# Moving the between-layer steps inside the attention loop of a two-layer kernel from eight places per phase to two

## The chip, the cores and the metric

The kernel runs on one core of a Trainium2 chip. The time is the device time of one execution in microseconds (us). The kernel before has a median of 1164.96 us over three runs (1164.99, 1161.2 and 1164.96).

## The reference, cut to what matters

The program is a stack of four blocks with a residual sum around each: attention, a mixture of experts, a state-space block and a second mixture of experts. Only the end of attention and what feeds the first mixture of experts matter here.

```python
x = x + attention(layernorm(x))            # 2 batches of 1024 tokens, 128 wide, 16 heads of 64
x = x + experts0(layernorm(x))             # below
x = x + state_space(layernorm(x))
x = x + experts1(layernorm(x))

def attention(x):
    Q, K, V = x @ W_Q + b_Q, x @ W_K + b_K, x @ W_V + b_V
    return softmax(Q @ K.T / 8) @ V @ W_O + b_O

def experts0(x):
    logits = (x @ wg_red.T) @ wg_unit.T                 # 8 experts
    scores, e = max(softmax(logits)), argmax(logits)    # one expert a token
    return scores * (gelu(x @ w1[e] + b1[e]) @ w2[e] + b2[e])
```

## The kernel before, in words

Attention is worked in 16 pairs of heads, pairs 0 to 7 for the first batch and 8 to 15 for the second. A pair has two phases, c = 0 and c = 1, one for each half of its 1024 queries. Every engine runs its own instructions strictly in the order of one list of steps, which `whole_order` writes out; a step is a name such as ("score", 3, 0, 5), and each engine takes from the list the steps in which it has a part. So a step's place in the list is its place on TensorE (PE), VectorE (DVE), ScalarE (ACT), GpSimd (POOL) and in the queue of SyncE (SP) at once. The line numbers below are those of the kernel before.

One phase, written by the function `phase`, is this:

- A head of eight rounds. In each, PE makes one product for the maxima of the next pair ("max", L605), which DVE reduces (L1507), and one block of scores of this pair ("score", L589 and L593), whose exponentials ACT takes (L1078). Maxima go through two slots of PSUM in turn and scores through two others. So the product for maxima number j has to wait until DVE has reduced number j-2, and the scores number j until ACT has taken the exponentials of number j-2. One of the two slots for maxima contains bank 7.
- A tail. PE multiplies the eight blocks of exponentials with the values ("pv" 0 to 7, L621). Between these products stand small steps: keys and queries of the pair after the next ("proj", L637, then k_lo or q_lo on DVE, L1500), in phases c = 1 a transposed row of maxima ("row", L660), the values of the next pair ("values", L652, taken by DVE with `valued`, L1536), and the sums of the softmax ("sumhalf", L671, taken by DVE, L1548). All of these use one bank of PSUM, bank 7, and each waits until the one before it has been read. "take" at the end is ACT's copy of the output to SBUF (L1087).
- POOL adds up the exponentials (L2020), seven additions a phase, all through the head and the tail; in the order of the list they come with the scores.

Into this loop the kernel also puts steps of the blocks around it: the layer norm of the second batch before attention (n = 1) and of the first batch before the experts (n = 2), and the routing of the first batch. Their parts are these.

- `lnvar` is 8 BN_STATS and 8 BN_AGGR on DVE (L1458, L1462). `lnroot` is four small instructions on POOL (L1967 to L1975). `lnrows` is 8 activations on ACT that write xrows (L1096), and it waits for `lnroot`. `lnturn` is 4 transposes on PE (L575) into bank 7, and `lncopy` reads them with ACT (L1040).
- `xr` is a matmul on PE (L703) into bank 7 and a copy on ACT; `logits` is 8 matmuls (L714) into bank 7, and `choose` six dependent instructions on DVE (L1603 to L1613), the second of which frees bank 7.
- `total` is 9 matmuls on PE (L725, L727) into bank 7. `count` in three parts (L1629 to L1660) is chains on DVE that end in the row numbers and the owners of slots. `scatter` is two indirect DMAs that POOL issues (L2031). `rate` is two small instructions on DVE.
- `rows`, `turn`, `turned` and `fetch` load the scattered rows, transpose them (PE into bank 7, then an ACT copy) and fetch the experts' weights (DMAs from SP's queue).

The table `EARLY` names the place of each such step. Before, its key is (pair, c, j): the steps go behind pv number j of that phase, j being one of 1, 3, 5, 6 and 7, and 7 meaning behind "take". `phase` puts them there as beside[1], beside[3] and so on. A second table, `LAST_EARLY`, does the same for the four pieces of the last pair.

Of the kernel before, what the change touches and what calls it, by code (L numbers as in the profile page):

```python
# [164 lines left out]
EARLY = {(3, 0, 1): [("lnvar", 1), ("lnroot", 1)], (3, 1, 3): [("lnrows", 1)], (4, 0, 5): [("lnturn", 1, 0), ("lncopy", 1, 0)],  # L165
         (4, 1, 6): [("lnturn", 1, 1), ("lncopy", 1, 1)], (5, 0, 1): [("bias", 1)],
         (8, 1, 1): [("lnvar", 2), ("lnroot", 2)], (9, 0, 3): [("lnrows", 2)], (9, 1, 6): [("lnturn", 2, 0), ("lncopy", 2, 0)],
         (10, 0, 5): [("lnturn", 2, 1), ("lncopy", 2, 1)], (10, 1, 6): [("xr", 0, 0), ("xr_out", 0, 0)], (11, 0, 5): [("xr", 0, 1), ("xr_out", 0, 1)],
         (11, 1, 1): [("logits", 0), ("choose", 0)], (12, 0, 1): [("expo", 0), ("alog",), ("total", 0), ("count", 0, 0)],
         (12, 0, 3): [("count", 0, 1)], (12, 1, 1): [("count", 0, 2)], (12, 1, 3): [("scatter", 0, 0), ("rate", 0)],  # L170
         (13, 0, 1): [("scatter", 0, 1)], (13, 0, 3): [("scatter", 0, 2)], (13, 0, 7): [("scatter", 0, 3)],
         (13, 1, 7): [("rows", 0, 0), ("rows", 0, 1)], (14, 0, 1): [("fetch", 0)], (14, 0, 5): [("turn", 0, 0), ("turned", 0, 0)],
         (14, 0, 7): [("fetch", 1), ("rows", 0, 2)], (14, 1, 1): [("fetch", 2)], (14, 1, 6): [("turn", 0, 1), ("turned", 0, 1)],
         (14, 1, 7): [("fetch", 3), ("rows", 0, 3)]}
# [2354 lines left out]
```

## Time and profile before

| what | value |
|---|---|
| median of three runs | 1164.96 us |
| the profiled execution | 1164.99 us |
| its span on the core | 1163.7 us |
| PE busy | 1096.0 us, 94% |
| DVE busy | 835.9 us, 72% |
| ACT busy | 619.0 us, 53% |
| POOL busy | 761.6 us, 65% |
| granted TensorE clock, mean | 0.985 |

The profiled execution took 1.3 us more than its span. Attention fills the span from about 45 to 734 us. In a row of the timeline the first number is the start in us from the span's start, the second the time from there to the end of the group, and what stands in brackets is how long the engine had been idle before it and what ended that. The clock is 1.00 at TensorE's level of 2.4 GHz and 0.50 at 1.2 GHz.

### The profile page before, as it was taken

To read this page: it belongs to the slowest core of one execution; us is meant where nothing else is said; L and a number is where in the kernel's file an instruction comes from. 1 tells how busy PE (TensorE), PEld (TensorE's weight loads), DVE (VectorE), ACT (ScalarE), POOL (GpSimd) and SP (SyncE) were. 2 spreads that over 40 slices of the span, in tenths; PEclk is the share of its full clock that TensorE was granted. 3 is DMA by queue.
4 is the path that set the end of the run, shared out by engine and by line. 5 is a ranking of instruction groups with operands and counts; after the bars stand their busy time and mean duration, and the time that the engine had idled before them with its cause. 6 is when DMAs were issued, how large, how long until landed. Compare 5 with 4: busy or idle time off the path is not lost.

```text
span 1163.7 us, 19598 instructions
## 1 busy us (share of the span) xinstructions
PE 1096.0 (94%) x7549; PEld 672.9 (58%) x7549; DVE 835.9 (72%) x1223; ACT 619.0 (53%) x867; POOL 761.6 (65%) x393
## 2 busy tenths in 40 slices
PE   5899999999999999999899999978879988899998
PEld 1456566566566565665556656877534434445786
DVE  4757668567577586576686755525799999998987
ACT  3535445445355355454334534545985665856753
POOL 3587869868868788777578980041389897995200
PEclk9999999999999999999899999989899999999999
DMA  6000000000000000000000215367464453451000
GB/s 204 2 1 2 1 1 1 2 1 2 1 2 1 2 1 1 2 1 1 1 1 11 69 39 184 97 179 219 153 207 155 146 163 130 142 163 38 11 10 18
DMA packets 38076, 68.85 MB, mean 59 GB/s; under 512 B 5952, under 2 KB 24128, under 8 KB 37984
## 3 DMA queue, kind: packets, MB, share of 16 engines
q1 hardware_dynamic: 34976, 64.52, 17.6%
q0 software_dynamic: 1024, 2.10, 0.6%
q8 instruction: 60, 0.98, 0.3%
q10 hardware_dynamic: 1984, 0.98, 0.3%
q14 instruction: 32, 0.26, 0.1%
HBM read 61.30 MB, written 6.16 MB: 58 GB/s over the span
## 4 chain that ended last, share of the span: by engine, by line
PE 76%; DVE 8%; issue 7%; POOL 5%; ACT 2%; DMA 2%; SPq 0%; POOLq 0%; DVEq 0%; ACTq 0%
PE psum L621 18%; PE psum L589 15%; PE psum L605 6%; PE psum L593 5%; PE psum L637 5%; PE psum L987 3%; PE psum L893 3%; PE psum L970 3%; PE psum L671 3%; POOL hc L2108 3%; PE psum L685 2%; PE psum L652 2%; PE psum L762 2%; PE psum L751 1%; DVE psum L1788 1%
## 5 line engine op out<-in xcount | busy, mean ns | idle before, releaser
L2020 POOL TENSOR_TENSOR psums<-psums,prob 128x1024 f32<-128x1024 f32 x180 | 427.8, 2376 | 26.7 <-POOL psums L2020 1.3
L1507 DVE TENSOR_REDUCE mx<-psum 128x2 f32<-128x1024 f32 x256 | 301.1, 1225 | 41.4 <-PE psum L605 41.0
L1078 ACT ACTIVATE prob<-psum 128x1024 f32<-128x1024 f32 x256 | 261.7, 1027 | 67.7 <-PE psum L593 42.8
L621 PE MATMUL psum<-prob,V 128*64 128x512 f32 x1024 | 248.9, 601 | 0.0
L2108 POOL TENSOR_TENSOR hc<-hs,cc 128x1024 f32<-128x1024 f32 x64 | 151.7, 2370 | 21.2 <-DVE hs L1795 18.7
L1795 DVE TENSOR_TENSOR_SCAN hs<-dA,psum 128x1024 f32<-128x1024 f32 x64 | 146.3, 2286 | 2.2
L2020 POOL TENSOR_TENSOR psums<-prob 128x1024 f32<-128x1024 f32 x30 | 72.2, 2407 | 115.5 <-ACT prob L1078 115.5
L621 PEld LDWEIGHTS psum<-prob,V 128*64 128x64 f32 x1024 | 67.9, 137 | 101.0 <-issue 97.2
L893 PE MATMUL psum<-hc,ident 128*128 128x512 f32 x256 | 123.3, 605 | 2.5 <-DVE slot_rows_h L1803 1.4
L605 PE MATMUL psum<-k_hi,q_hi 64*128 64x512 f32 x512 | 108.9, 414 | 4.5 <-DVE mx L1507 1.6
L589 PE MATMUL psum<-q_hi,k_hi 64*128 64x512 f32 x512 | 106.8, 404 | 0.0
L593 PE MATMUL psum<-guard,row_one 64*128 64x512 f32 x512 | 103.8, 391 | 0.7 <-DMA guard<-mrow 0.7
L589 PE MATMUL psum<-q_hi,k_lo 64*128 64x512 f32 x512 | 103.8, 391 | 0.0
L589 PE MATMUL psum<-q_lo,k_hi 64*128 64x512 f32 x512 | 103.5, 391 | 0.0
L1087 ACT COPY oraw<-psum 128x512 f32<-128x512 f32 x32 | 18.8, 587 | 145.3 <-PE psum L621 145.3
L1562 DVE SCALAR_TENSOR_TENSOR x<-psum,inv,x 128x128 f32<-128x128 f32 x256 | 72.0, 344 | 21.4 <-PE psum L685 15.5
L605 PEld LDWEIGHTS psum<-k_hi,q_hi 64*128 64x128 f32 x512 | 50.9, 186 | 42.1 <-issue 26.8
L893 PEld LDWEIGHTS psum<-hc,ident 128*128 128x128 f32 x256 | 48.5, 193 | 44.6 <-issue 32.4
L877 PE MATMUL psum<-xdr,pickr 128*128 128x512 f32 x128 | 57.7, 532 | 10.8 <-DVE hs L1795 10.6
L589 PEld LDWEIGHTS psum<-q_hi,k_hi 64*128 64x128 f32 x512 | 49.0, 185 | 32.2 <-ACT prob L1078 17.9
L1052 ACT ACTIVATE q_hi<-psum,bq 128x512 fp32r<-128x512 f32 x32 | 22.0, 688 | 83.7 <-PE psum L637 83.7
L1300 ACT ACTIVATE dA<-slotT,alog 128x1024 f32<-128x1024 f32 x32 | 36.6, 1149 | 40.0 <-DVE hs L1795 39.7
(287 smaller groups left out, 1736.3 us busy)
## 6 DMA issues: line engine op xcount, KB each, us to landing
cc<-C_rows SPq DMA_DIRECT2D x64, 512.0 KB, 3.7
kq_wts<-in_e_rows SPq DMA_DIRECT2D x14, 578.0 KB, 4.8
e_wts<-in_e_rows SPq DMA_DIRECT2D x10, 578.0 KB, 4.0
e_w<-in_e_rows SPq DMA_DIRECT2D x6, 578.0 KB, 4.7
slots_in<-e_zero SPq DMA_DIRECT2D x2, 960.0 KB, 8.2
slots_out<-e_y SPq DMA_DIRECT2D x30, 64.0 KB, 2.5
x<-in_x SPq DMA_DIRECT2D x2, 512.0 KB, 4.9
e_w<-in_e_w SPq DMA_DIRECT2D x1, 1024.0 KB, 7.8
```

Of the source, the lines that this page charges most:

```text
L589: pe.matmul(both[:, s, :], left[HALF[s], js], right[HALF[s], cs], start=(part == 0), stop=False)
L593: ins = pe.matmul(both[:, s, :], A.row_one[HALF[s], :], A.guard[q][HALF[s], cs], start=False, stop=True)
L605: ins = pe.matmul(both[:, s, :], A.q_hi[r][HALF[s], t * P:(t + 1) * P], A.k_hi[r][HALF[s], c * CH:(c + 1) * CH], start=True, stop=True)
L621: ins = pe.matmul(A.O[HALF[s], :], A.V[pair % 2][:, j, s * DH:(s + 1) * DH], A.prob[unit(pair, c, j) % NPB][:, s * CH:(s + 1) * CH], start ...
L637: ins = pe.matmul(bank[HALF[s], :], w[:, (2 * p + s) * DH:(2 * p + s + 1) * DH], K.xnT[:, b, c * CH:(c + 1) * CH], start=True, stop=True)
L893: ins = pe.matmul(X.Y[:, c * CH:(c + 1) * CH], K.ident[:, :], X.hc[u % 3][:, c * CH:(c + 1) * CH], start=(u > 0 and n == 0), stop=(n == NS ...
L1078: act.activation(A.prob[n % NPB][:, :], slots.bank("score", pair, c, j).rearrange("p s n -> p (s n)"), ACT.Exp, scale=float(DH) ** -0.5).t ...
L1507: dve.tensor_reduce(K.A.mx[:, :, t, c], slots.bank("max", pair, t, c), AXX, ALU.max).then_inc(*slots.inc("max", pair, t, c))
L1562: ins = dve.scalar_tensor_tensor(out=K.x[:, tile, :], in0=slots.bank("out", pair, c)[:, s, t * P:(t + 1) * P], scalar=A.inv[:, s * NT + 4 ...
L1795: dve.tensor_tensor_scan(X.hs[u % 3][:, :], X.dA[u % 3][:, :], X.gain[u % 2], 0.0, ALU.mult, ALU.add).then_inc(X.state_done, 1)
L2020: pool.tensor_tensor(total[:, :], (K.A.prob[(n - 1) % NPB] if j == 1 else total)[:, :], K.A.prob[n % NPB][:, :], ALU.add).then_inc(*K.psum ...
L2108: pool.tensor_tensor(X.hc[u % 3][:, :], X.hs[u % 3][:, :], X.cc[u % NCC][:, :], ALU.mult).then_inc(X.product_done, 1)
```

## The change: what it does

The key of `EARLY` becomes (pair, i), with i from 0 to 3, two places in each phase. i = 0 and 2 are the first place of c = 0 and of c = 1: behind the values of the next pair and pv 5, or in c = 1 behind pv 5 and the values of the next pair, and ahead of pv 6. i = 1 and 3 are the place behind "take", which is the end of the phase. `LAST_EARLY` goes into the same table, with the same steps as before. The sums ("sumhalf") now always come between pv 6 and pv 7; before, they came behind pv 7 in the four phases that had a step behind pv 6. No step is added or taken away, and no instruction changes its form.

```diff
-EARLY = {(3, 0, 1): [("lnvar", 1), ("lnroot", 1)], (3, 1, 3): [("lnrows", 1)], (4, 0, 5): [("lnturn", 1, 0), ("lncopy", 1, 0)],
-         (4, 1, 6): [("lnturn", 1, 1), ("lncopy", 1, 1)], (5, 0, 1): [("bias", 1)],
...
-LAST_EARLY = {0: [("turn", 0, 2), ("turned", 0, 2)] + [("fetch", n) for n in range(4, 8)],
...
+EARLY = {(3, 0): [("lnvar", 1), ("lnroot", 1)], (3, 1): [("lnrows", 1)], (3, 2): [("lnturn", 1, 0), ("lncopy", 1, 0)],
+         (3, 3): [("lnturn", 1, 1), ("lncopy", 1, 1)], (4, 0): [("bias", 1)],
...
 def phase(pair, c):
-    beside = [EARLY.get((pair, c, j), []) for j in range(NT)]
+    early = [EARLY.get((pair, 2 * c + i), []) for i in range(2)]
...
-    order += first[:1] + pv[:1] + first[1:] + pv[1:2] + beside[1] + pv[2:3] + second[:1] + pv[3:4] + second[1:] + beside[3] + pv[4:5]
+    order += first[:1] + pv[:1] + first[1:] + pv[1:3] + second[:1] + pv[3:4] + second[1:] + pv[4:5]
     if c == NC - 1:
-        added = [("sumhalf", pair, 0)]
-        order += [("row", nxt), ("rowed", nxt)] + pv[5:6] + [("values", nxt, 1), ("valued", nxt, 1)]
+        order += [("row", nxt), ("rowed", nxt)] + pv[5:6] + [("values", nxt, 1), ("valued", nxt, 1)] + early[0] + pv[6:7] + [("sumhalf", pair, 0)]
     else:
-        added = [("sumhalf", last, NC - 1)] * (last >= 0)
-        order += [("values", nxt, 0), ("valued", nxt, 0)] + pv[5:6] + beside[5]
-    if beside[6]:
-        order += pv[6:7] + beside[6] + pv[7:] + added
-    else:
-        order += pv[6:7] + added + pv[7:]
-    return order + [("take", pair, c)] + beside[7]
+        order += [("values", nxt, 0), ("valued", nxt, 0)] + pv[5:6] + early[0] + pv[6:7] + [("sumhalf", last, NC - 1)] * (last >= 0)
+    return order + pv[7:] + [("take", pair, c)] + early[1]
```

The places of all moved steps, as (pair, c, pv behind which they stand), "end" being behind "take" and "5+" behind pv 5 and the values:

| step | before | now |
|---|---|---|
| lnvar 1, lnroot 1 | 3, 0, 1 | 3, 0, 5+ |
| lnrows 1 | 3, 1, 3 | 3, 0, end |
| lnturn/lncopy 1, first and second half | 4, 0, 5+ and 4, 1, 6 | 3, 1, 5+ and 3, 1, end |
| bias 1 | 5, 0, 1 | 4, 0, 5+ |
| lnvar 2, lnroot 2 | 8, 1, 1 | 9, 0, 5+ |
| lnrows 2 | 9, 0, 3 | 9, 0, end |
| lnturn/lncopy 2 | 9, 1, 6 and 10, 0, 5+ | 9, 1, 5+ and 9, 1, end |
| xr 0 | 10, 1, 6 and 11, 0, 5+ | 10, 1, 5+ and 10, 1, end |
| logits, choose | 11, 1, 1 | 11, 1, end |
| expo, alog, total, count 0 | 12, 0, 1 | 12, 0, 5+ |
| count 1 | 12, 0, 3 | 12, 0, end |
| count 2 | 12, 1, 1 | 12, 1, 5+ |
| scatter 0, rate | 12, 1, 3 | 12, 1, end |
| scatter 1, 2, 3 | 13, 0, 1; 13, 0, 3; 13, 0, end | 13, 0, 5+; 13, 0, end; 13, 1, 5+ |
| fetch 0; fetch 2 | 14, 0, 1; 14, 1, 1 | 14, 0, 5+; 14, 1, 5+ |
| turn/turned, second | 14, 1, 6 | 14, 1, 5+ |

ACT around the end of the phase (3, 0), in the kernel before. oraw is "take", prob the exponentials, xrows `lnrows`, xnT `lncopy`:

```order
L1087 COPY oraw<-psum 128x512
L1078 ACTIVATE prob<-psum 128x1024 x8
L1052 ACTIVATE k_hi<-psum,bk 128x512
L1052 ACTIVATE q_hi<-psum,bq 128x512
L1096 ACTIVATE xrows<-x,shift,rstd 128x128 x8
L1087 COPY oraw<-psum 128x512
```

The same place now:

```order
L1081 COPY oraw<-psum 128x512
L1090 ACTIVATE xrows<-x,shift,rstd 128x128 x8
L1072 ACTIVATE prob<-psum 128x1024 x8
L1046 ACTIVATE k_hi<-psum,bk 128x512
L1046 ACTIVATE q_hi<-psum,bq 128x512
L1034 COPY xnT<-psum 128x512
L1081 COPY oraw<-psum 128x512
L1034 COPY xnT<-psum 128x512
```

The eight activations of `lnrows` moved from behind the exponentials of the phase (3, 1) to ahead of them.

DVE in the phase (11, 1), in the kernel before. nmx ends the head, x is the output's update, e_top to e_onehot is `choose`, mrow the row, V the values, inv the sums:

```order
L1517 TENSOR_REDUCE nmx<-mx 128x2x8
L1562 SCALAR_TENSOR_TENSOR x<-psum,inv,x 128x128 x8
L1500 SCALAR_TENSOR_TENSOR k_lo<-psum,bk,k_hi 128x512
L1603 TENSOR_REDUCE e_top<-psum 128x8
L1605 TENSOR_TENSOR e_shifted<-psum,e_top 128x64
L1607 TENSOR_SCALAR e_onehot<-e_shifted 128x64
L1609 TENSOR_TENSOR e_onehot<-e_onehot,e_rank 128x64
L1611 TENSOR_REDUCE e_top<-e_onehot 128x8
L1613 TENSOR_TENSOR e_onehot<-e_onehot,e_top 128x64
L1500 SCALAR_TENSOR_TENSOR q_lo<-psum,bq,q_hi 128x512
L1525 CAST mrow<-psum 128x128
L1536 TENSOR_TENSOR V<-psum,bv 128x512
```

The same engine now, from the values of (11, 1) to the first maxima of (12, 0):

```order
L1530 TENSOR_TENSOR V<-psum,bv 128x512
L1542 RECIPROCAL inv<-psum 128x2x4
L1597 TENSOR_REDUCE e_top<-psum 128x8
L1599 TENSOR_TENSOR e_shifted<-psum,e_top 128x64
L1601 TENSOR_SCALAR e_onehot<-e_shifted 128x64
L1603 TENSOR_TENSOR e_onehot<-e_onehot,e_rank 128x64
L1605 TENSOR_REDUCE e_top<-e_onehot 128x8
L1607 TENSOR_TENSOR e_onehot<-e_onehot,e_top 128x64
L1501 TENSOR_REDUCE mx<-psum 128x2 x8
```

`choose` moved from between k_lo and q_lo to ahead of the maxima of the next phase.

## Rows read from the trace of the kernel before

**Rows 1.** Timeline of ACT: the copy that ends a phase (start, length, what).
```profile
406.59 0.59 ACT L1087 COPY oraw<-psum 128x512 f32<-128x512 f32 x1 [5.49 <-PE psum L621]
...
428.24 0.59 ACT L1087 COPY oraw<-psum 128x512 f32<-128x512 f32 x1 [6.06 <-PE psum L621]
...
449.29 0.59 ACT L1087 COPY oraw<-psum 128x512 f32<-128x512 f32 x1 [2.41 <-PE psum L621]
...
493.33 0.59 ACT L1087 COPY oraw<-psum 128x512 f32<-128x512 f32 x1 [2.23 <-PE psum L621]
...
538.33 0.59 ACT L1087 COPY oraw<-psum 128x512 f32<-128x512 f32 x1 [2.23 <-PE psum L621]
...
568.11 0.59 ACT L1087 COPY oraw<-psum 128x512 f32<-128x512 f32 x1 [11.65 <-PE psum L621]
...
593.24 0.59 ACT L1087 COPY oraw<-psum 128x512 f32<-128x512 f32 x1 [6.78 <-PE psum L621]
```

**Rows 2.** Timeline around the head of the phase (3, 1), all engines.
```profile
191.47 0.50 PE L605 MATMUL psum<-k_hi,q_hi 64*128 64x512 f32 x2
...
191.62 0.25 POOL L1967 TENSOR_SCALAR std<-mv 128x8 f32<-128x8 f32 x1
...
192.01 9.44 DVE L1507 TENSOR_REDUCE mx<-psum 128x2 f32<-128x1024 f32 x8 [1.13 <-PE psum L605]
...
192.93 4.52 ACT L1078 ACTIVATE prob<-psum 128x1024 f32<-128x1024 f32 x4 [0.76 <-PE psum L593]
...
194.01 0.19 PEld L589 LDWEIGHTS psum<-q_hi,k_hi 64*128 64x128 f32 x2 [0.17 <-ACT prob L1078]
...
194.05 0.20 POOL L1975 TENSOR_TENSOR shift<-shift,rstd 128x8 f32<-128x8 f32 x1
...
195.19 2.40 POOL L2020 TENSOR_TENSOR psums<-prob 128x1024 f32<-128x1024 f32 x1 [0.94 <-ACT prob L1078]
...
207.07 3.18 ACT L1096 ACTIVATE xrows<-x,shift,rstd 128x128 f32<-128x128 f32 x8
```

**Rows 3.** Timeline of the tail of (9, 1): PE free, and DVE's values.
```profile
467.83 1.03 PE L621 MATMUL psum<-prob,V 128*64 128x512 f32 x4
468.04 0.69 DVE L1536 TENSOR_TENSOR V<-psum,bv 128x512 f32<-128x512 f32 x1 [1.60 <-PE psum L652]
468.88 0.63 PE L575 MATMUL psum<-ident,xrows 128*128 128x128 f32 x4
```

**Rows 4.** Timeline of (11, 1): logits, `choose` on DVE, additions on POOL.
```profile
549.53 9.84 POOL L2020 TENSOR_TENSOR psums<-psums,prob 128x1024 f32<-128x1024 f32 x4
...
551.93 1.92 PE L714 MATMUL psum<-e_wgu,xnT 128*128 128x8 f32 x16 [0.47 <-DVE k_lo L1500]
...
554.63 2.33 DVE L1609 TENSOR_TENSOR e_onehot<-e_onehot,e_rank 128x64 f32<-128x64 f32 x1
...
557.26 2.20 DVE L1613 TENSOR_TENSOR e_onehot<-e_onehot,e_top 128x64 f32<-128x64 f32 x1
...
560.26 0.45 PE L660 MATMUL psum<-ident,nmx 128*128 128x128 f32 x1 [2.82 <-DVE q_lo L1500]
```

**Rows 5.** Timeline of DVE: `choose` of the second batch, POOL idle.
```profile
752.93 0.23 DVE L1603 TENSOR_REDUCE e_top<-psum 128x8 f32<-128x64 f32 x1 [2.29 <-PE psum L714]
...
754.19 0.22 DVE L1613 TENSOR_TENSOR e_onehot<-e_onehot,e_top 128x64 f32<-128x64 f32 x1
```

**Rows 6.** Stretches: length, busy time (instructions) by engine, PEclk, DMA share, GB/s.
```profile
560.00:566.00 6.00, 5.74 (x31) 3.06 (x31) 1.10 (x3) 0.00 (x0) 0.00 (x0) 0.50 0.02 4
...
796.00:800.00 4.00, 3.25 (x19) 2.43 (x20) 1.84 (x8) 1.27 (x3) 0.00 (x0) 1.00 0.51 165
...
870.00:874.00 4.00, 3.50 (x9) 2.44 (x10) 3.04 (x3) 3.30 (x6) 3.83 (x3) 0.57 0.40 126
```

**Rows 7.** Timeline of PE: the gaps ahead of 796.38 and 870.50 us.
```profile
796.38 0.66 PE L575 MATMUL psum<-ident,xrows 128*128 128x128 f32 x4 [3.11 <-DVE xrows L1479]
...
870.50 1.11 PE L575 MATMUL psum<-ident,xrows 128*128 128x128 f32 x4 [2.56 <-ACT xrows L1112]
```

More of the change, by code:

```diff
@@ L159 @@
     pass
-EARLY = {(3, 0, 1): [("lnvar", 1), ("lnroot", 1)], (3, 1, 3): [("lnrows", 1)], (4, 0, 5): [("lnturn", 1, 0), ("lncopy", 1, 0)],
-         (4, 1, 6): [("lnturn", 1, 1), ("lncopy", 1, 1)], (5, 0, 1): [("bias", 1)],
[L167 to L174, printed above, removed]
@@ L175 @@
-LAST_EARLY = {0: [("turn", 0, 2), ("turned", 0, 2)] + [("fetch", n) for n in range(4, 8)],
-              1: [("turn", 0, 3), ("turned", 0, 3), ("fetch", 8), ("fetch", 9)], 2: [("fetch", 10), ("fetch", 11)], 3: [("fetch", 12)]}
+EARLY = {(3, 0): [("lnvar", 1), ("lnroot", 1)], (3, 1): [("lnrows", 1)], (3, 2): [("lnturn", 1, 0), ("lncopy", 1, 0)],
+         (3, 3): [("lnturn", 1, 1), ("lncopy", 1, 1)], (4, 0): [("bias", 1)],
+         (9, 0): [("lnvar", 2), ("lnroot", 2)], (9, 1): [("lnrows", 2)], (9, 2): [("lnturn", 2, 0), ("lncopy", 2, 0)],
+         (9, 3): [("lnturn", 2, 1), ("lncopy", 2, 1)], (10, 2): [("xr", 0, 0), ("xr_out", 0, 0)], (10, 3): [("xr", 0, 1), ("xr_out", 0, 1)],
+         (11, 3): [("logits", 0), ("choose", 0)], (12, 0): [("expo", 0), ("alog",), ("total", 0), ("count", 0, 0)],
+         (12, 1): [("count", 0, 1)], (12, 2): [("count", 0, 2)], (12, 3): [("scatter", 0, 0), ("rate", 0)],
+         (13, 0): [("scatter", 0, 1)], (13, 1): [("scatter", 0, 2)], (13, 2): [("scatter", 0, 3)],
+         (13, 3): [("rows", 0, 0), ("rows", 0, 1)], (14, 0): [("fetch", 0), ("turn", 0, 0), ("turned", 0, 0)],
+         (14, 1): [("fetch", 1), ("rows", 0, 2)], (14, 2): [("fetch", 2), ("turn", 0, 1), ("turned", 0, 1)],
+         (14, 3): [("fetch", 3), ("rows", 0, 3)], (15, 0): [("turn", 0, 2), ("turned", 0, 2)] + [("fetch", n) for n in range(4, 8)],
+         (15, 1): [("turn", 0, 3), ("turned", 0, 3), ("fetch", 8), ("fetch", 9)], (15, 2): [("fetch", 10), ("fetch", 11)],
+         (15, 3): [("fetch", 12)]}
@@ L243, in last_phase @@
         order += [("out", pair - 1, 0), ("out", pair - 1, 1)]
-    second = ([("sumhalf", pair, 0)] if f == 3 else []) + LAST_EARLY[f]
+    second = ([("sumhalf", pair, 0)] if f == 3 else []) + EARLY.get((pair, f), [])
     pv = [("pv", pair, c, j) for j in js]
```

## The prediction

> **What bounds the kernel now.** I read the page's busy shares first (the table above): PE 94% of the span, the other engines 53 to 72%. In the timeline of attention PE goes from one product to the next nearly without a gap. So there a microsecond in which PE waits is a microsecond of the end, and work that another engine does beside PE costs nothing until PE waits for it. Next I took the copies that end the phases [rows 1], since they show what each moved step costs today. A phase with nothing put into it takes 428.24 - 406.59 = 21.65 us for c = 1 and 449.29 - 428.24 = 21.05 us for c = 0 (in this one `lnrows` ran, and cost nothing). A pair makes 42.70 us. Against that:
>
> - the layer norm 2, two phases from 449.29 to 493.33: 44.04 - 42.70 = 1.3 us (the layer norm 1 has the same parts, and I price it alike);
> - `xr`, two phases to 538.33: 45.00 - 42.70 = 2.3 us;
> - `logits` and `choose`, (11, 1): 29.78 - 21.65 = 8.1 us;
> - `total` and two parts of `count`, (12, 0): 25.13 - 21.05 = 4.1 us.
>
> Last I read the timeline engine by engine where a step leaves and where it arrives [rows 2 to 5]. The head of a phase has no room on ACT: the second pair of scores after the first waits for the first exponentials and is released with 0.17 us of idle time [rows 2]. On DVE there is a little room: the reductions of maxima begin 192.01 - 191.47 = 0.54 us behind the first product and take 9.44 / 8 = 1.18 us each [rows 2], while the third product follows two rounds of 1.16 us behind the first, so DVE may start about 0.55 us late before PE stands.
>
> **The change, part by part.** The sum is made against the profiled execution, 1164.99 us, which is 1.3 us above its span and equals the median of 1164.96 within 0.03 us.
>
> *lnrows behind "take", twice.* This is the largest term. ACT would be ready for the first exponentials of (3, 1) at 192.93. In front of them now stand eight activations, which first wait for `lnroot`. POOL comes to `lnroot` only after its seven additions of (3, 0): it starts at 191.62 and ends at 194.05 + 0.20 = 194.25 [rows 2]. Moving `lnvar` later on DVE doesn't delay that: behind the values DVE still ends it about 0.5 us ahead of 191.6 (I reckon with 8 + 8 instructions of some 0.15 us). The eight activations take 3.18 us [rows 2]: 194.3 + 3.2 = 197.5. So the first exponentials come 197.45 - 192.93 = 4.5 us late. Behind them on ACT are all eight exponentials of the phase; PE stands at its third scores, with the slots full, and has no other work in its order. Exponentials (1.13 us each) and rounds of PE (1.16 us) run at nearly the same pace, so nothing is won back: 4.5 us. The same holds at (9, 0), where POOL's root moves too: its additions end there 0.2 us behind the phase's end, as they do here. Two times 4.5 = 9.0 us. What hid these activations before was the tail, in which ACT has little to do.
>
> *Bank 7 behind the values, four times* (the first halves of lnturn 1 and 2, `xr` and the second `turn`, all at c = 1). Before, one pv stood between the values and the step. Now the step waits for DVE to read the values: PE is free at 467.83, DVE reads until 468.04 + 0.69 = 468.73 [rows 3], and the hop to PE adds 0.1 to 0.2 us: 1.0 us each. All four: 4.1 us. Their own work on PE stays as it was.
>
> *Behind "take" with PE's part, four times* (the second halves of the two lnturn and of `xr`, and `logits`). ACT's copy ends ahead of the first exponentials, and bank 7 is read ahead of the second product for maxima, so only PE's own time counts: 0.63 us for four transposes [rows 3], about 1.0 us for the matmul of `xr`. The same work cost about as much before, so both layer norms and `xr` get 0. With the other parts: layer norms +9.0 + 2.1, `xr` +1.0, `turn` +1.0.
>
> *logits and choose to the end of (11, 1).* Before, 8.1 us: 1.9 of matmuls and a wait of 0.5 [rows 4], 2.8 of idle PE until q_lo released bank 7 for the row [rows 4], and the rest, about 3 us, at half clock: PEclk is 0.50 from 560 to 566 us [rows 6]. `choose` is slow there because of two instructions: L1609 takes 2.33 us and L1613 2.20 us for 64 elements, and they end at 556.96 and 559.46, each 0.1 us behind the end of an addition of POOL (549.53 + 3 x 2.46 = 556.91 and + 4 x 2.46 = 559.37) [rows 4]. For the second batch, with POOL idle, the whole chain takes 754.19 + 0.22 - 752.93 = 1.5 us [rows 5]. Behind "take" POOL is idle: its additions end about when the phase does, and the next one waits for the second exponentials, 3.5 us into the head (195.19 against 191.47, released by the exponentials) [rows 2]. So I take 1.5 us, not 5.5. DVE then begins the maxima 1.9 + 0.1 + 1.5 = 3.5 us behind the last pv, which is 1.6 us behind the first product instead of 0.55; less the room of 0.55 PE stands for 0.5 us. Cost now 1.9 + 0.5 = 2.4 us, against 8.1: -5.7 us. The Trainium skill ("SBUF — State Buffer", Who interferes with whom) says that a VectorE instruction with two SBUF inputs and a GpSimd instruction that reads SBUF shut each other out, and that whoever starts first keeps the port for its whole length. The two slow rows agree with it (2.33 and 2.20 us against 0.22 us). By this rule the new place gives the 2.4 us above; without it the chain would keep its 5.5 us, which is the first rival.
>
> *total and count.* The matmuls of `total` are nine small ones like the eight of `logits` with 1.9 us [rows 4]; with the ninth and a break between two pv I take 2.4 us. `count` part 0 now lies under pv 6, the sums and pv 7; part 1, 1.3 us when it isn't held up, comes behind the sums and eats the room of DVE but not more. Bounds: 2.4 if all of it is hidden, 4.7 if both of its slow instructions stay slow. I take 2.4 against 4.1: -1.7 us. `count` part 2, `rate`, `bias`, the scatters and the fetches: each moves within reach of idle time on DVE, POOL or SP; bounds -0.5 and +0.5 together, taken as -0.4 (part 2 no longer holds up q_lo). Scatter 3 now ends some 3 us into (14, 0), and the load of its rows is needed 13 us later.
>
> *The clock.* Two new gaps of 4.5 us. In the trace a gap of 2.8 us ahead of 560.26 was followed by six us at 0.50 [rows 4, 6], and one of 2.6 us ahead of 870.50 by four us at 0.57 on the average [rows 6, 7]. I count a fall after each. PE loses half of the time it works at 0.50: 1.6 us for the short fall, 3 for the long one; I take 2.2 each: +4.4 us. Bounds 0 and 6.8.
>
> **Sum:** 9.0 + 4.1 - 5.7 - 1.7 - 0.4 + 4.4 = +9.7; the break in the tail that goes away where a step leaves c = 0 gives back about 0.3 us twice, -0.6: +9.1. 1164.99 + 9.1 = 1174.1 us.
>
> **The rivals.**
>
> 1. *`choose` and `count` stay slow at the head.* Then DVE starts the maxima of (12, 0) 5.6 us behind the first product, and PE stands 4.45 us instead of 0.5; (12, 1) starts late by another 2.3 us; a third fall of the clock adds about 2.2. 1174.1 + 4.0 + 2.3 + 2.2 = 1182.6. For it: the only rows of `choose` inside attention are slow. Against it: both slow ones end with an addition of POOL, and POOL is idle at the new place. 12%.
> 2. *The clock stays up.* 1174.1 - 4.4 = 1169.7. For it: a gap of 3.1 us ahead of 796.38 was followed by no fall [rows 6, 7]. Against it: the new gaps are 1.4 us longer than that one, and two shorter ones were followed by a fall. 12%.
> 3. *The other side: not slower.* The activations of `lnrows` don't reach PE, at the heads of (3, 1) and (9, 1). If ACT finished them ahead of the first scores, both stalls and both falls would be gone: 1174.1 - 9.0 - 4.4 = 1160.7, since the 8.1 us at (11, 1) are a real loss which the change takes away. It decides from the point where POOL's root ends 3.2 us ahead of 192.9. For it: nothing but that POOL might run ahead of its order in the trace. Against it: POOL has additions without a gap until 191.6. 7%.
>
> **How the numbers follow.** The forecast, two stalls with falls and a quick `choose`, gets 62%, its own range being 1170 to 1179 from the bounds of the clock. The remaining 7% is for stretches behind attention where gaps of PE meet the clock differently, some 3 us either way. The predicted time is 1174. The range 1165 to 1182 leaves out most of rivals 1 and 3. A change of 0.5%, 5.8 us, is what a measurement of this kernel can tell: slower means above 1170.8, faster below 1159.1. Slower: the forecast nearly whole, rival 1 and a part of rival 2, 0.74. Within 0.5%: rivals 2 and 3 for the most part, 0.22. Faster: 0.04.
>
> **What would show it.** In the profile of the changed kernel: the phases that follow `lnrows` ((3, 1) and (9, 1)) 6 us or more longer than 21.65, with ACT's xrows right behind oraw and idle until POOL's shift; PEclk near 0.5 for some us there; the transposes of (9, 1) with a wait of about 1 us for V; L1603 and L1607 (the old L1609 and L1613) at 0.22 us, and (11, 1) back at 21.6; no fall of the clock at (11, 1). I am wrong if the first exponentials of (3, 1) start less than 2 us behind oraw, if the two instructions of `choose` still take 2 us, or if PEclk stays 1.00 through both stalls.

## The result, and the profile after

The changed kernel has a median of 1172.65 us (1172.04 to 1174.8, 4 runs), the kernel before beside it 1164.32 us (1161.2 to 1164.99, 4 runs). The ratio is 1.0078, 95% interval 1.0056 to 1.0099: slower by 8.3 us. The profiled execution took 1174.9 us, its span is 1173.6 us (before 1163.7), and the mean granted clock 0.983 (0.985).

All line numbers of the changed kernel are 6 lower than those of before. First the copies that end phases on ACT, as in [rows 1]; the ends are those of (2, 1), (3, 0), (3, 1), (9, 0), (9, 1), (11, 0), (11, 1) and (12, 0):

```profile
170.22 0.59 ACT L1081 COPY oraw<-psum 128x512 f32<-128x512 f32 x1 [6.06 <-PE psum L615]
...
191.27 0.59 ACT L1081 COPY oraw<-psum 128x512 f32<-128x512 f32 x1 [5.49 <-PE psum L615]
...
221.45 0.59 ACT L1081 COPY oraw<-psum 128x512 f32<-128x512 f32 x1 [2.22 <-PE psum L615]
...
456.65 0.59 ACT L1081 COPY oraw<-psum 128x512 f32<-128x512 f32 x1 [5.49 <-PE psum L615]
...
485.71 0.59 ACT L1081 COPY oraw<-psum 128x512 f32<-128x512 f32 x1 [2.22 <-PE psum L615]
...
553.05 0.59 ACT L1081 COPY oraw<-psum 128x512 f32<-128x512 f32 x1 [5.49 <-PE psum L615]
...
574.72 0.59 ACT L1081 COPY oraw<-psum 128x512 f32<-128x512 f32 x1 [6.06 <-PE psum L615]
...
601.52 0.59 ACT L1081 COPY oraw<-psum 128x512 f32<-128x512 f32 x1 [7.55 <-PE psum L615]
```

Their differences are the lengths of the phases. The table gives all phases that differ in any of the kernels shown, in us; every other phase is the same within 0.1 us in all of them.

| phase | before | changed | e1 | e2 | e3 | e4 | e7 | e6 | e8 | e12 |
|---|---|---|---|---|---|---|---|---|---|---|
| (3, 1) | 21.64 | 30.18 | 23.07 | 28.71 | 21.64 | 28.95 | 27.45 | 21.28 | 21.64 | 21.64 |
| (4, 0) | 21.93 | 21.67 | 21.68 | 21.89 | 21.88 | 21.66 | 21.68 | 22.99 | 21.93 | 21.90 |
| (4, 1) | 21.32 | 21.64 | 21.64 | 21.28 | 21.29 | 21.65 | 21.64 | 21.68 | 21.32 | 21.30 |
| (5, 0) | 21.97 | 21.07 | 21.07 | 21.94 | 21.94 | 21.08 | 21.07 | 21.08 | 21.96 | 21.93 |
| (9, 1) | 21.27 | 29.06 | 23.04 | 23.47 | 21.27 | 27.65 | 27.59 | 21.27 | 21.24 | 21.27 |
| (10, 0) | 22.77 | 21.65 | 21.68 | 22.77 | 22.76 | 21.65 | 21.69 | 22.99 | 22.76 | 22.76 |
| (10, 1) | 21.79 | 23.56 | 23.54 | 21.75 | 21.76 | 23.56 | 23.59 | 21.75 | 21.75 | 21.74 |
| (11, 0) | 23.21 | 22.13 | 22.12 | 23.22 | 23.23 | 22.10 | 22.10 | 23.42 | 23.21 | 23.22 |
| (11, 1) | 29.78 | 21.67 | 21.63 | 27.04 | 21.65 | 21.63 | 21.62 | 21.63 | 27.03 | 21.65 |
| (12, 0) | 25.13 | 26.80 | 28.40 | 25.15 | 30.24 | 25.72 | 25.76 | 25.74 | 23.38 | 25.77 |
| (12, 1) | 22.13 | 21.62 | 21.64 | 22.14 | 22.12 | 21.62 | 21.64 | 21.60 | 22.09 | 20.45 |
| (14, 1) | 19.57 | 21.38 | 21.34 | 19.54 | 19.58 | 21.36 | 21.33 | 19.56 | 19.57 | 19.57 |
| (15, 0) | 19.92 | 19.04 | 19.00 | 19.88 | 19.92 | 19.04 | 19.00 | 19.92 | 19.87 | 19.91 |

(The phases (13, 0) to (14, 0) have a paragraph of their own at the end.) The copy that ends a phase waits for pv 7 and not for the sums. So a phase whose sums stand behind pv 7 counts about 1 us short by this measure, and the next one about 1 us long, as (9, 1) and (10, 0) before: such phases are to be read together. Changed less before: layer norm 1, four phases, +7.7; layer norm 2 +6.7; `xr` +0.7; `logits` and `choose`, with `total` and `count`, -8.1, +1.7 and -0.5; the second `turn` +0.9. That is +9.0 us. Behind attention it is 1.2 us more, which can't be put down to the change: that stretch took 427.0 to 432.4 us in the profiles of before, changed and e1 to e4, in no order that follows the moved steps.

Around the head of (3, 1), to be held against [rows 2] (start, length, idle time before in brackets):

```profile
193.72 0.20 POOL L1969 TENSOR_TENSOR shift<-shift,rstd 128x8 f32<-128x8 f32 x1
...
193.96 3.19 ACT L1090 ACTIVATE xrows<-x,shift,rstd 128x128 f32<-128x128 f32 x8 [2.11 <-POOL shift L1969]
...
197.05 1.91 ACT L1072 ACTIVATE prob<-psum 128x1024 f32<-128x1024 f32 x2
...
199.98 0.63 PE L599 MATMUL psum<-k_hi,q_hi 64*128 64x512 f32 x2
...
200.65 1.23 DVE L1501 TENSOR_REDUCE mx<-psum 128x2 f32<-128x1024 f32 x1 [5.42 <-PE psum L599]
```

ACT is idle 2.11 us for POOL's shift, the first exponentials come 197.05 - 191.27 = 5.78 us behind oraw, where it was 192.93 - 191.59 = 1.34 us before (191.59 being the same copy in that trace), so 4.44 us later. The clock there and at (9, 1), and where the routing now stands (length, busy time of PE, PEld, DVE, ACT and POOL, PEclk, DMA share, GB/s):

```profile
194.00:198.00 4.00, 0.00 (x0) 0.00 (x0) 1.23 (x2) 4.00 (x10) 0.00 (x0) 0.93 0.00 0
198.00:202.00 4.00, 3.89 (x18) 3.15 (x20) 1.23 (x1) 1.99 (x3) 2.82 (x2) 0.50 0.00 0
202.00:206.00 4.00, 4.00 (x28) 3.06 (x28) 2.53 (x3) 2.43 (x3) 3.86 (x2) 0.72 0.00 0
462.00:466.00 4.00, 2.40 (x12) 1.96 (x14) 0.00 (x0) 2.76 (x5) 1.47 (x1) 0.71 0.00 0
574.00:578.00 4.00, 4.00 (x26) 3.14 (x24) 1.12 (x7) 0.59 (x1) 0.18 (x1) 0.79 0.00 0
578.00:582.00 4.00, 4.00 (x30) 3.09 (x28) 3.69 (x4) 2.26 (x3) 0.24 (x1) 0.79 0.00 0
```

PE does nothing for four microseconds (its idle time there is 4.15 us, and 4.26 us at (9, 1)) and then works at the lower level, 1.2 GHz, from 198 to 202 us. The last two rows are a third fall, ahead of which PE had not been idle (busy 4.00 of 4.00 us, and 3.97 in the four before). In the tail of (9, 1), as in [rows 3]:

```profile
481.39 0.69 DVE L1530 TENSOR_TENSOR V<-psum,bv 128x512 f32<-128x512 f32 x1 [1.60 <-PE psum L646]
...
482.23 0.63 PE L569 MATMUL psum<-ident,xrows 128*128 128x128 f32 x4 [0.89 <-DVE V L1530]
```

PE waits 0.89 us for the values. And `choose` behind the end of (11, 1), against [rows 4]:

```profile
574.61 2.08 PE L708 MATMUL psum<-e_wgu,xnT 128*128 128x8 f32 x16
...
576.72 0.23 DVE L1597 TENSOR_REDUCE e_top<-psum 128x8 f32<-128x64 f32 x1 [2.71 <-PE psum L708]
...
577.47 0.22 DVE L1603 TENSOR_TENSOR e_onehot<-e_onehot,e_rank 128x64 f32<-128x64 f32 x1
577.98 0.22 DVE L1607 TENSOR_TENSOR e_onehot<-e_onehot,e_top 128x64 f32<-128x64 f32 x1
578.13 1.22 DVE L1501 TENSOR_REDUCE mx<-psum 128x2 f32<-128x1024 f32 x1
...
581.76 2.41 POOL L2014 TENSOR_TENSOR psums<-prob 128x1024 f32<-128x1024 f32 x1 [7.57 <-ACT prob L1072]
```

Both slow instructions take 0.22 us, and POOL is idle throughout the chain.

### The profile page after: what moved, and what is told of

It is laid out like the page before. It is cut to its first block, busy times and chain, and to the rows that moved or that the text cites. A ratio compares the mean times of both kernels' runs of the same rounds, so it can differ in the third digit from the quotient of the medians.

```text
span 1173.6 us, 19598 instructions
## 1 busy us (share of the span) xinstructions
PE 1099.0 (94%) x7549; PEld 676.2 (58%) x7549; DVE 828.6 (71%) x1223; ACT 619.2 (53%) x867; POOL 761.6 (65%) x393
## 4 chain that ended last, share of the span: by engine, by line
PE 73%; POOL 8%; issue 7%; DVE 7%; ACT 3%; DMA 2%; POOLq 0%; SPq 0%; ACTq 0%; DVEq 0%
PE psum L615 18%; PE psum L583 14%; PE psum L599 5%; PE psum L631 5%; PE psum L587 5%; PE psum L981 3%; PE psum L887 3%; POOL psums L2014 3%; PE psum L964 3%; PE psum L665 2%; POOL hc L2102 2%; PE psum L679 2%; PE psum L646 2%; DVE mx L1501 2%; PE psum L756 2%
## 5 line engine op out<-in xcount | busy, mean ns | idle before, releaser
L615 PE MATMUL psum<-prob,V 128*64 128x512 f32 x1024 | 246.4, 597 | 0.0
L1494 DVE SCALAR_TENSOR_TENSOR q_lo<-psum,bq,q_hi 128x512 fp32r<-128x512 f32 x28 | 21.0, 751 | 60.8 <-ACT q_hi L1046 60.8
```

Source lines behind the costliest of these rows:

```text
L615: ins = pe.matmul(A.O[HALF[s], :], A.V[pair % 2][:, j, s * DH:(s + 1) * DH], A.prob[unit(pair, c, j) % NPB][:, s * CH:(s + 1) * CH], start ...
```

## The experiments

Times are compared within the set in which kernels ran side by side; the kernel before had 1163.08 us beside e1 to e4, 1169.58 beside e5 to e8, 1170.58 beside e9 and e10, and 1163.21 beside e11 and e12. The times that the expectations give were worked out from 1163 us; in the sets where the kernel before took 1170 us the ratio is what can be held against them. In those two sets the phase (13, 1) was also shorter in kernels that have it as changed (22.6 us in e6, e7 and e10) than in those that have it as before (24.27 in e5 and e8, 25.83 in e9), where in before, changed and e1 to e4 it took 21.65 us in all; so the ratios of e6, e7 and e10 probably hold a gain of 1.7 us or more that isn't the moved steps' elsewhere.

**e1, lnrows back in the tail.** The changed kernel with `lnrows` taken out of the table and put ahead of pv 4 at c = 1, where the normalised rows are still in time for the first transposes:

```diff
+TAIL = {(3, 1): [("lnrows", 1)], (9, 1): [("lnrows", 2)]}
-    order += ... + pv[3:4] + second[1:] + pv[4:5]
+    order += ... + pv[3:4] + second[1:] + TAIL.get((pair, c), []) + pv[4:5]
```

> The changed kernel with one part undone: the eight activations of lnrows (1 and 2) stand behind pv 3 and its q_lo in the tails of (3, 1) and (9, 1) again, all else as changed. Theory (exponentials stand behind lnrows on ACT, and PE behind them): both stalls of 4.1 to 4.5 us and both stretches at half clock go, the phases (3, 1) and (9, 1) shrink from 30.2 and 29.1 us to 23.2 or 23.3 us (21.65 and 1.6 for the transposes with their wait), so about 13 us less than the changed kernel: 1159 to 1161 us, which is 3 to 5 us below the kernel before. Rival (the phases are long because of the transposes and their waits at the same place, not because of lnrows): they stay above 27 us and the time stays at 1169 us or more.

Measured: 1161.26 us (10 runs), 0.9977 of before (0.9963 to 0.9990). (3, 1) and (9, 1) fell to 23.07 and 23.04 us. So those two places cost 7.1 + 6.0 = 13.1 us, more than the whole loss, and without them the change is a small gain. The whole came down by less, 8.3 + 1.8 = 10.1 us by the two differences from before, and stayed just above the 1159 to 1161 us expected; 1.6 us of that is (12, 0), where the fall of the clock behind the logits was longer than in the changed kernel (28.40 against 26.80 us).

**e2, lnrows alone.** The kernel before with two entries moved:

```diff
-(3, 1, 3): [("lnrows", 1)]      (9, 0, 3): [("lnrows", 2)]
+(3, 0, 7): [("lnrows", 1)]      (9, 0, 7): [("lnrows", 2)]
```

> The kernel before with one part of the change alone: lnrows 1 behind take of (3, 0), where POOL's lnroot is still to come, and lnrows 2 behind take of (9, 0), where lnroot 2 was done a phase earlier. Theory: at (3, 1) PE stands 4.1 to 4.5 us for the third scores and the clock falls, the phase takes 27.5 to 29.5 us instead of 21.6; at (9, 1) the wait for POOL is missing, so the first exponentials come only 2.4 us late (3.2 us of activations less the 0.8 us that ACT waits for scores anyway), the phase takes 23.7 us without and up to 26 us with a fall of the clock. Together 8 to 12 us above the kernel before, 1172 to 1176 us. Rival (it is only the wait for POOL that costs, and the activations alone hide): (9, 1) stays at 21.3 us and the sum is 6 to 8 us.

Measured: 1173.2 us (5 runs, from 1167.74 to 1173.82), 1.0073 of before (1.0046 to 1.0099). Its loss can't be told from that of the whole change. The profiled execution is the fastest of the five, and has (11, 1) at 27.04 instead of 29.78 us, so what the slower ones lost beside this isn't shown. (3, 1) took 28.71 us, as expected. At (9, 1), where `lnroot` is already done, POOL holds nothing up, and the price is the activations' alone:

```profile
456.32 3.18 ACT L1096 ACTIVATE xrows<-x,shift,rstd 128x128 f32<-128x128 f32 x8
...
459.41 1.91 ACT L1078 ACTIVATE prob<-psum 128x1024 f32<-128x1024 f32 x2
...
460.46 0.50 PE L589 MATMUL psum<-q_hi,k_hi 64*128 64x512 f32 x2 [1.93 <-ACT prob L1078]
```

PE idles 1.93 us, the clock stays at 1.00, and the phase is 2.2 us longer (23.47). The changed kernel's stall at this place costs 4.55 us (see e7); the rest of it is the wait for POOL's root. The rival, that the activations alone hide, is out.

**e3, choose alone.** The kernel before with one entry moved:

```diff
-(11, 1, 1): [("logits", 0), ("choose", 0)]
+(11, 1, 7): [("logits", 0), ("choose", 0)]
```

> The kernel before with one part of the change alone: logits and choose behind take of (11, 1). Theory (choose is slow only while POOL adds): the two instructions take 0.22 us each, (11, 1) takes 21.65 instead of 29.8 us, and (12, 0) takes 2.0 to 2.5 us more for the matmuls and the room of DVE, and 1.5 us more if the clock falls as in the changed kernel: 4 to 6 us less than before, 1158.5 to 1160.5 us. Rival (the work of choose costs PE the same wherever it stands): (12, 0) grows by 5 us or more and the time stays within 2 us of the kernel before.

Measured: 1160.91 us (10 runs), 0.9984 (0.9970 to 0.9998). Both slow instructions take 0.23 us now, and (11, 1) is back at 21.65 us as expected, but (12, 0), where `total` and `count` still have their old places, went from 25.13 to 30.24 us. That is 5.1 us more and not the 2.0 to 4.0 expected; the rival had 5 us or more, but for the work of `choose`, and here it is other instructions that are slow. Its rows:

```profile
573.12 7.34 POOL L2020 TENSOR_TENSOR psums<-psums,prob 128x1024 f32<-128x1024 f32 x3
573.21 2.30 DVE L1775 TENSOR_SCALAR alog<-alog 128x32 f32<-128x32 f32 x1
...
575.89 2.17 DVE L1631 TENSOR_TENSOR e_cmp<-e_place,e_steps 128x64 f32<-128x64 f32 x1
...
578.35 2.15 DVE L1636 TENSOR_TENSOR_SCAN e_ctile<-e_all,e_ntile 128x8 f32<-128x8 f32 x1
...
580.73 0.75 DVE L1500 SCALAR_TENSOR_TENSOR q_lo<-psum,bq,q_hi 128x512 fp32r<-128x512 f32 x1
...
581.54 1.98 PE L652 MATMUL psum<-wv,xnT 128*64 128x128 f32 x16 [2.37 <-DVE q_lo L1500]
```

POOL's three additions, taken singly, end at 575.47, 577.98 and 580.47 us, and three small instructions of DVE end at 575.51, 578.06 and 580.50: each is held until an addition ends. Before, two instructions of that phase were caught (2.04 and 1.71 us). So with `logits` and `choose` ahead of it the same chain met the additions differently, and three were caught: q_lo comes late, PE idles 2.37 us, and the clock falls there (PEclk 0.66 from 582 to 586 us).

**e4, filler in the stall.** The changed kernel, in which the product for the third maxima at the heads of (3, 1) and (9, 1) is made ten times:

```diff
+REPEAT = {(4, *MAXES[NT + 2]): 9, (10, *MAXES[NT + 2]): 9}
-    for s in range(2):
+    for s in [*range(2)] * (1 + REPEAT.get((pair, t, c), 0)):
```

> The changed kernel, with the product for the third maxima at the heads of (3, 1) and (9, 1) made ten times over instead of once (the same product into the same slot), so that PE works through most of the stall. Theory (the stall costs 4.1 to 4.5 us for itself and, apart from that, the clock falls because PE stood idle): the stalls of PE's scores stay, PEclk stays 1.00 there, (3, 1) takes 26.5 to 27 us instead of 30.2 and (9, 1) 27 instead of 29.1: 4.5 to 5.5 us less than the changed kernel, 1167 to 1168.5 us. Rival (the clock's fall is not what lengthens these phases, or falls whatever PE does): the phases stay within 0.5 us of 30.2 and 29.1, or grow, and the time is 1172 us or more.

Measured: 1173.03 us (4 runs), 1.0075 of before (1.0048 to 1.0103), no better than the changed kernel. The 20 matmuls took 2.44 us, 0.12 us each, too little to fill the stall, and left PE idle for 2.10 us, and 2.26 at (9, 1); a short fall came at (3, 1) and none at (9, 1). The time of the whole missed my expectation and was what the rival gave. The phases, 28.95 and 27.65 us, were 1.2 and 1.4 us shorter than in the changed kernel, more than the rival allows, but as PE still stood idle they didn't settle it, so the filler was made longer.

**e7, the filler longer.** The same with 17 in place of 9.

> This is the changed kernel with the product for the third maxima at the heads of (3, 1) and (9, 1) made 18 times instead of 10, 36 matmuls of 0.12 us, which fill the stall of 4.5 us without making it longer. Theory (the falls of the clock in the changed kernel come from PE's standing still and cost 2.5 and 1.4 us): PEclk 1.00 through both heads, (3, 1) and (9, 1) both 27.65 us, time about 4 us below that of the changed kernel, 1168 to 1170 us, if the rest of the program is as it was there. Rival (the fall is not what the stall costs): the phases stay at 29 to 30 us.

Measured: 1172.53 us (10 runs) beside 1169.58, ratio 1.0028 (1.0019 to 1.0038). The time is above the 1168 to 1170 us expected, since before took more in this set; the ratio is 0.5%, 5.8 us, below that of the changed kernel, where 4 were expected.

```profile
192.07 4.27 PE L602 MATMUL psum<-k_hi,q_hi 64*128 64x512 f32 x36
192.48 3.19 ACT L1093 ACTIVATE xrows<-x,shift,rstd 128x128 f32<-128x128 f32 x8 [2.11 <-POOL shift L1972]
196.63 0.50 PE L586 MATMUL psum<-q_hi,k_hi 64*128 64x512 f32 x2 [0.29 <-ACT prob L1075]
```

```profile
194.00:198.00 4.00, 3.71 (x34) 2.85 (x32) 1.23 (x1) 3.61 (x8) 0.44 (x1) 1.00 0.00 0
198.00:202.00 4.00, 4.00 (x38) 3.23 (x36) 3.89 (x4) 3.53 (x4) 3.86 (x2) 1.00 0.00 0
```

The stall is as long as before, now filled with useless products; the clock stays at 1.00, and the phases take 27.45 and 27.59 us. So the falls in the changed kernel cost 30.18 - 27.45 = 2.7 us and 29.06 - 27.59 = 1.5 us, and the stall itself the rest: 27.45 - 23.07 = 4.4 and 27.59 - 23.04 = 4.55 us.

**e5, POOL's additions made short.** The kernel before with POOL's additions of (11, 1) cut to 64 columns; the sums of that phase are incomplete.

```diff
+    w = 64 if (pair, c) == (11, 1) and j > 1 else 2 * CH
-    pool.tensor_tensor(total[:, :], ...
+    pool.tensor_tensor(total[:, 0:w], ...
```

> This is the kernel before with POOL's last six additions of the phase (11, 1) cut to 64 columns of the 1024, so that this phase's sums of exponentials are left out of the output for the most part. Theory (an addition of POOL that is under way holds up a DVE instruction with SBUF operands): L1609 and L1613 of choose take about 0.22 us instead of 2.33 and 2.20, PE no longer idles 2.8 us ahead of the row, the clock stays up, and (11, 1) takes 24 to 24.5 us instead of 29.78. Rival (the two instructions are slow for what they are, or for the tail they stand in): they stay above 2 us and the phase stays above 28.5 us.

Measured: 1165.61 us in one run.

```profile
553.23 0.23 DVE L1609 TENSOR_TENSOR e_onehot<-e_onehot,e_rank 128x64 f32<-128x64 f32 x1
...
553.74 0.23 DVE L1613 TENSOR_TENSOR e_onehot<-e_onehot,e_top 128x64 f32<-128x64 f32 x1
```

At their old place in the tail the two instructions take 0.23 us, a tenth of [rows 4]; PE has no gap ahead of the row. The rival is false: it is POOL's long additions that hold DVE. The phase took 25.86 us, not 24 to 24.5; the clock fell behind the logits here (0.82 and 0.84 from 550 to 560 us), and the expectation had none.

**e8, total and count alone.** The kernel before with the entry (12, 0, 1) at (12, 0, 5) and (12, 0, 3) at (12, 0, 7).

> This is the kernel before with two entries moved alone: expo, alog, total and count 0 from (12, 0, 1) to (12, 0, 5), and count 1 from (12, 0, 3) to behind take. Theory of the prediction: (12, 0) goes from 25.13 to about 23.4 us, 1.7 us off, 1162.5 to 1164 us. Rival (the chain of count is as slow at the new place, since POOL's additions run through the tail too, and now it holds up the sums or the next maxima): (12, 0) 25 to 28 us and the time the same or up to 3 us more.

Measured: 1165.92 us (9 runs), 0.9978 (0.9963 to 0.9993), and (12, 0) at 23.38 us, just the 23.4 expected. The interval, 0.8 to 4.3 us less than before, holds the 1.7 expected:

```profile
586.39 0.23 DVE L1629 COPY e_place<-psum 128x72 f32<-128x72 f32 x1 [1.91 <-PE psum L727]
586.66 0.36 DVE L1631 TENSOR_TENSOR e_cmp<-e_place,e_steps 128x64 f32<-128x64 f32 x1
...
587.30 0.17 DVE L1636 TENSOR_TENSOR_SCAN e_ctile<-e_all,e_ntile 128x8 f32<-128x8 f32 x1
```

The last addition of the phase ends at 586.93 us, so of `count` only L1631 is still touched (0.36 us). The other one touched is `alog` (L1775), 0.50 us here and ending 0.03 us behind an addition, against 0.25 in the kernel before.

**e6, bank 7 apart.** e1, and in the pairs 3, 9, 10 and 14 the first place of c = 1 behind pv 6, the sums behind pv 7, as before:

```diff
+        if pair in (3, 9, 10, 14):
+            return order + pv[6:7] + early[0] + pv[7:] + [("sumhalf", pair, 0), ("take", pair, c)] + early[1]
```

> This is e1_rows_in_tail (the changed kernel with lnrows back in the tails) and beside it the first halves of lnturn 1 and 2, of xr and the second turn again behind pv 6 instead of ahead of it, in (3, 1), (9, 1), (10, 1) and (14, 1). Theory (each of these four steps pays for a wait on bank 7 of 0.9 us behind the values, less the break in the tail that it saves): the wait for V ahead of the transposes is gone, (10, 1) goes from 23.54 to about 22.6 us, (3, 1) and (9, 1) from 23.05 to about 22.1, (14, 1) from 21.34 to about 20.5; in all 3.5 us off, 1157 to 1159 us where e1 had 1161.26, faster than both kernels. Rival (the wait only moves: the transposes' bank is then late for the sums, as in the kernel before, where these pairs of phases cost 1.3 and 2.3 us): 0 to 1.5 us off, 1160 to 1161 us.

Measured: 1163.74 us (5 runs) beside 1169.58, ratio 0.9949 (0.9934 to 0.9964), faster than both kernels by their ratios. But of the gain against e1 only 2.3 us lies in the four pairs of phases (0.5 three times and 0.9), between the 3.5 of the theory and the 1.5 of the rival; the rest is mainly (12, 0), where e1 had a fall of the clock (28.40 against 25.74 us). The two rows at the end of (9, 1) tell where the 0.9 us go:

```profile
468.28 1.05 PE L672 MATMUL psum<-ones,psums 128*64 128x1 f32 x32
...
469.73 0.63 PE L576 MATMUL psum<-ident,xrows 128*128 128x128 f32 x4 [0.40 <-DVE inv L1549]
```

With the sums at the end, the second transposes wait 0.40 us for DVE to read them, and so do the second ones of the layer norm 1 and the second `xr`. Three waits of 0.40 us take the place of four of 0.89: 2.4 us less, where 2.3 came.

**e9, the routing alone.** The kernel before with four entries moved: `logits` and `choose` to (11, 1, 7), `total` and `count` 0 to (12, 0, 5), `count` 1 to (12, 0, 7), `count` 2 to (12, 1, 6).

> This is the kernel before with the routing of the first batch alone moved: logits and choose behind take of (11, 1), total and count 0 to (12, 0, 5), count 1 behind take of (12, 0), count 2 behind pv 6 of (12, 1). The layer norms and xr stay. Theory (the change joins a good part, the routing, with a bad part, lnrows behind take and bank 7 behind the values; (12, 0) had its 28 to 30 us in e1 and e3 from a fall of the clock or from count in its old place): (11, 1) 21.65 us, (12, 0) about 25.75 (28.4 if the clock falls behind logits), (12, 1) about 21.6; 8.0 us less than before in all, 0.991 to 0.995 of it. Rival (the moved chains meet other additions of POOL again, as in e3): (12, 0) or (12, 1) over 27 us, ratio 0.996 to 1.0.

Measured: 1163.07 us (6 runs) beside 1170.58, ratio 0.9945 (0.9931 to 0.9960). (11, 1), (12, 0) and (12, 1) took 21.64, 25.73 and 20.43 us. The 1.2 us by which (12, 1) is below the 21.6 expected is for the most part no gain: `count` 2 behind pv 6 puts the sums behind pv 7, and (13, 0) took 21.99 us instead of 21.08. The routing's part of the change is a gain by itself.

**e10, the changed kernel once more.**

> This is the changed kernel, word for word, profiled in a second execution beside e9, to see what belongs to its order and what to the execution. If the order sets the falls of the clock at the two stalls, (3, 1) and (9, 1) take 29 to 30.2 us again. If the fall behind the logits belongs to the order too, (12, 0) takes 26.8 us again; if to the execution, as its absence in e4, e6 and e7 says, 25.75 us or 28.4 us can come as well. (13, 1) took 21.66 us in the changed kernel and 22.6 in e6 and e7; if that is not the order's either, it may differ here. Ratio to before 1.006 to 1.010.

Measured: 1178.42 us (4 runs) beside 1170.58, ratio 1.0080 (1.0061 to 1.0098). (3, 1) 29.99, (9, 1) 28.95, (12, 0) 26.81 us: the two falls at the stalls come again, and so does the third.

**e11, the kernel before once more.**

> This is the kernel before, word for word, profiled once more, for the phase (13, 1): it took 21.66 us in the first seven profiles and 22.6 (four scatters at the phase's head: e6, e7, e10) or 24.3 to 25.8 us (six scatters there: e5, e8, e9) in the last six. If that belongs to the chip on which a set ran, this run shows 24 to 26 us where the kernels beside it show a long (13, 1) too, and it accounts for a part of the 6 us by which the kernel before was slower in those sets. If it belongs to the moved steps, it shows 21.66 us wherever it runs.

Measured: 1163.3 us in one run, (13, 1) at 21.64 us, in a set where no kernel had a long (13, 1); so it doesn't say what makes it long in the others. But e5 has every step just where this kernel has it and took 24.27 us there, so the moved steps alone don't account for it. It showed something else: (11, 1) took 27.05 us, as in e2 and e8, and not the 29.78 on which the prediction rests.

**e12, routing and scatters.** e9 with scatter 0 and `rate` at (12, 1, 7), scatter 1 at (13, 0, 5), 2 at (13, 0, 7), 3 at (13, 1, 6).

> This is e9_before_with_routing_moved with the scatters and rate where the changed kernel has them: scatter 0 and rate behind take of (12, 1), scatter 1 at (13, 0, 5), scatter 2 behind take of (13, 0), scatter 3 behind pv 6 of (13, 1). If the long (13, 1) comes from six scatters on POOL at its head, which make ACT and DVE start late there, four of them cost less: (13, 1) 22.6 us where e9 had 25.8, about 3 us off on such a chip and 0 where the phase takes 21.66 us anyway; ratio to before 0.990 to 0.995. Rival (scatter 0 at the head of (13, 0) only moves the loss there): (13, 0) 23 to 24 us, ratio the same as that of e9, 0.9945.

Measured: 1156.42 us (12 runs) beside 1163.21, ratio 0.9952 (0.9935 to 0.9968): the lowest time of all, 6.8 us below the kernel before on the same chip. The question it was made for stays open: in this set (13, 1) is short with six DMAs too (21.64 us in e11). The phases (13, 0), 21.97 us, and (13, 1), 20.50, with (14, 0), 20.94, differ from before by where the sums stand; (13, 0) was the same in e9, with scatter 0 in its old place. Against e9 the ratio can't be told apart.

## Why the prediction was right

The forecast was 1174 us (1174.1 by its sum) and slower; 1172.65 us and slower by 0.8% came, and 1174.9 us in the profiled execution. Step by step:

- *lnrows, 9.0 us.* Measured 4.4 and 4.55 us (e7 less e1), 8.95 in all, by the mechanism named: ACT idle until POOL's shift, then eight activations ahead of the first exponentials. e2 splits one of them into 2.2 us for the activations and the rest for the wait. Rival 3 is out.
- *Bank 7, 4.1 us, and -0.6 for the break.* The mechanism came, the size was too large. The wait was 0.89 us, 3.6 in all four. As a net price it is less: over the phases that the steps left and reached, e1 is above the kernel before by 0.6 us (layer norm 1), 0.7 (layer norm 2), 0.7 (`xr`) and 0.8 (`turn`), 2.8 in all, where 3.5 were forecast. So about 0.8 us are saved where the steps left, and no run takes that apart. "The same work cost about as much before" holds: in the kernel before PE has no wait above 0.15 us in any of these phases, and the 0.40 us of e6 are its own.
- *logits and choose, -5.7 us.* Measured: (11, 1) -8.11, and their cost at (12, 0) 25.76 - 23.38 = 2.38 (e7 less e8), against 2.4 forecast: -5.7. The reason is shown by e5, by POOL's additions alone. The rule of the Trainium skill ("SBUF — State Buffer", Who interferes with whom), that a VectorE instruction with two SBUF inputs and a GpSimd instruction that reads SBUF shut each other out, agrees with the 0.23 us where the additions are short and the 2.33 and 2.20 us where they are long. Rival 1 is out. What was not forecast: the four profiles that keep the old place whole show 29.78 us once and 27.03 to 27.05 us three times (e2, e8, e11). In these three the clock fell sooner, behind the logits, and for half as long (in e11 PEclk 0.68 from 555 to 560 us); PE's slower work took up a part of its wait, 1.13 to 1.19 us instead of the 2.82 of [rows 4], and the fall cost less than that of [rows 6]. Against those the move is worth 3.0 us. Beside e5, which had such a fall too and took 25.86 us, the held instructions cost PE only 1.2 us there. How often an execution has the 29.78 us isn't known.
- *total and count, -1.7 us.* Measured 23.38 - 25.13 = -1.75 (e8). *count 2 and the rest, -0.4.* Measured -0.51 at (12, 1).
- *The clock, +4.4 us.* Falls came at both stalls, 2.7 and 1.5 us (e7): 4.2. Rival 2 is out. The long fall and the short one of the two rows I had averaged both came. A third, which no step had, costs 26.80 - 25.76 = 1.0 us at (12, 0).
- *Two readings that were wrong and cost nothing.* The phase taken as one with nothing in it, (8, 1), holds `lnvar` 2; (7, 1), which has nothing, took 21.65 us as well. And BN_STATS takes 0.28 us and not 0.15; still POOL's shift starts 193.72 - 191.27 = 2.45 us behind the copy now and started 194.05 - 191.59 = 2.46 us behind it before.

In the profiled pair it adds up: 8.95 + 4.2 + 1.0 + 2.8 - 5.7 - 1.75 - 0.5 = 9.0, the 9.0 measured in attention. The mechanisms of the forecast are those that came; that the sum came so near owes something to luck, since the missed third fall (1.0 us) and the too large terms for bank 7 and the clock (0.7 and 0.2) cancel.

## What to carry to other kernels

Work that is free in a tail can cost its full length at a head: ask of each new place what is queued behind the step on its engine, and which engine must be done before it, here POOL, which is busy with its additions to the end of the phase. Price a group of moves one by one, since this change was a gain of 8 us and a loss of 17 in one; e9 and e12 keep only the first. And look for small VectorE instructions that end just as a long GpSimd one does: the same chain had two of them caught in the kernel before, three in e3 and none for more than 0.36 us in e8.
